# Later casts and subtractions for the second batch's turned queries and keys in a differential attention block

## The reference, cut to what matters

```
q = (query @ Wq).reshape(b, t, 32, 16);  k the same;  v = (query @ Wv).reshape(b, t, 16, 2, 16)
q = apply_rotary_interleaved(q, cos, sin);  k the same      # o1 = x1*c - x2*s, o2 = x1*s + x2*c
attn1 = softmax(causal(q1 k1^T * scale)) @ [v1, v2];  attn2 the same with q2, k2
attn  = irfft((rfft(attn1) - lambda * rfft(attn2)) * gaussian)   # along t
attn  = attn * rsqrt(mean(attn^2) + eps) * rms_weight * (1 - lambda_init)
x = x + attn.reshape(b, t, 512) @ Wout                      # then the other three blocks
```

## Time and profile before

| | us |
|---|---|
| median of 3 runs | 1260.25 (1258.77 to 1263.32) |
| profiled execution | 1260.45 |
| its span | 1258.7 |
| busy in the span: PE, DVE, ACT, POOL | 1127.6, 811.5, 618.0, 800.6 |
| busy from 180 to 900 us: PE, DVE, ACT, POOL | 629.26, 415.39, 440.50, 579.87 |

### The profile page before, as it was taken

How to read it: one execution, slowest core, us unless ns; L and a number is a source line. 1 busy time by engine, 2 the same in 40 slices (tenths; PEclk the granted TensorE clock), 3 DMA queues, 4 the chain that set the end, 5 groups by cost and what they waited for, 6 DMA issues and landing times. The chain is left out here.

```text
span 1258.7 us, 20791 instructions
## 1 busy us (share of the span) xinstructions
PE 1127.6 (90%) x7603; PEld 639.1 (51%) x7618; DVE 811.5 (64%) x1345; ACT 618.0 (49%) x1009; POOL 800.6 (64%) x584
## 2 busy tenths in 40 slices
PE   6999967989689889889898898897899999999996
PEld 5888722333234343343243243342367888887764
DVE  6887175565564665656557646643288788787786
ACT  4444215657557657656666564666642233332321
POOL 2012159569969879869879789668215677667321
PEclk9999959899889999999999998998999999999999
DMA  8333340120231220220221203103332322233651
GB/s 273 98 126 109 90 116 26 51 68 26 67 78 41 68 68 26 68 68 26 69 68 39 58 21 109 30 1 129 107 110 96 131 84 94 92 101 116 222 197 51
DMA packets 74836, 107.55 MB, mean 85 GB/s; under 512 B 12912, under 2 KB 36592, under 8 KB 74736
## 3 DMA queue, kind: packets, MB, share of 16 engines
q1 hardware_dynamic: 63616, 79.35, 21.4%
q0 software_dynamic: 4064, 14.16, 2.9%
q10 hardware_dynamic: 7056, 12.72, 2.7%
HBM read 68.44 MB, written 37.75 MB: 84 GB/s over the span
## 5 line engine op out<-in xcount | busy, mean ns | idle before, releaser
L1090 DVE TENSOR_REDUCE nm<-score 128x1 f32<-128x640 f32 (+6 forms) x352 | 349.4, 1025 | 272.6 <-PE score L981 220.8
L1257 POOL TENSOR_TENSOR base<-base,plain 128x2048 f32<-128x2048 f32 (+2 forms) x78 | 301.0, 3860 | 16.1 <-ACT plain L1206 6.2
L1206 ACT ACTIVATE plain<-score 128x1024 f32<-128x1024 f32 (+3 forms) x288 | 207.2, 734 | 108.4 <-PE score L997 60.4
L992 PE MATMUL score<-q,k 98*128 98x512 bf16 (+7 forms) x768 | 194.9, 340 | 51.7 <-ACT plain L1206 21.1
L992 PEld LDWEIGHTS score<-q,k 98*128 98x128 bf16 (+1 forms) x768 | 55.0, 99 | 155.1 <-DVE nm L1090 58.0
L1206 ACT ACTIVATE base<-score 128x1024 f32<-128x1024 f32 x96 | 97.5, 1023 | 72.9 <-PE score L997 51.6
L1010 PE MATMUL acc<-plain,vg 128*32 128x512 f32 (+3 forms) x1152 | 114.4, 470 | 0.0
L976 PE MATMUL score<-k,q 48*128 48x512 bf16 (+3 forms) x512 | 70.5, 355 | 17.7 <-DVE nm L1090 17.5
L1612 PE MATMUL m_b<-m_winh,m_hTh 128*128 128x512 f32 x192 | 83.6, 435 | 1.6 <-DVE m_k L1902 1.6
L1612 PE MATMUL m_b<-m_winh,m_hTl 128*128 128x512 f32 x192 | 75.8, 395 | 0.0
L1612 PE MATMUL m_b<-m_winl,m_hTh 128*128 128x512 f32 x192 | 75.7, 394 | 0.0
(11 more groups left out here) (312 smaller groups left out, 2514.3 us busy)
## 6 DMA issues: line engine op xcount, KB each, us to landing
q<-piece_scratch SPq DMA_DIRECT2D x192, 64.0 KB, 2.7
k<-piece_scratch SPq DMA_DIRECT2D x192, 64.0 KB, 2.3
piece_scratch<-n_pieces SPq DMA_DIRECT2D x16, 384.0 KB, 3.0
piece_scratch<-pieces POOLq DMA_DIRECT2D x8, 768.0 KB, 4.0
n_x1in<-in_query SPq DMA_DIRECT2D x16, 256.0 KB, 3.6
v_scratch<-n_v ACTq DMA_DIRECT2D x16, 256.0 KB, 2.2
vg<-v_scratch SPq DMA_DIRECT2D x8, 512.0 KB, 4.4
att_scratch<-m_qT SPq DMA_DIRECT2D x8, 512.0 KB, 3.0
```

The lines of the kernel that those rows point to most:

```text
L992: mm = nc.tensor.matmul(score[k % RING][:, x, t0:HALF], kst[n % SLOTS][c, first + x, j * P:(j + 1) * P], qst[n % SLOTS][c, first + x, h * ...
L1090: nc.vector.tensor_reduce(out, src, AX.X, ALU.max, negate=True).then_inc(s_max, 1)
L1206: nc.scalar.activation(tile_of(n, v)[:, first:first + 2, t0:HALF], score[k % RING][:, :, t0:HALF], ACT.Exp)\
L1257: nc.gpsimd.tensor_tensor(total, total, tile_of(n, v)[:, :, t0:HALF], ALU.add)\
```

## The change

Four of the five distances in `ROTATE` grow. Nothing else is altered, and every unit has the same operations as before.

```
-ROTATE = (('rotate', 0, 4), ('cast', 0, 12), ('rotate', 1, 15), ('cast', 1, 17), ('rotate', 2, 19))
+ROTATE = (('rotate', 0, 4), ('cast', 0, 14), ('rotate', 1, 17), ('cast', 1, 23), ('rotate', 2, 26))
```

## The result

Timed in turn with the kernel before, 20 executions each, the changed kernel takes 1266.1 us (1261.92 to 1267.7) and the kernel before 1258.93 us (1257.22 to 1263.86). The ratio is 1.0047, 95% interval 1.0036 to 1.0058: slower by 5.9 us, between 4.5 and 7.3 (the medians by themselves lie 7.2 us apart). That is resolved, and just within the 0.5%, 6.3 us, that the prediction called no change; the interval reaches past it. 1262.6 us was forecast, in a range from 1255 to 1268 us. The profiled execution took 1266.95 us, its span 1265.2 us, 6.5 us more than before.

A forecast was written before the change was run, and what follows sets the result against it. Bounds: POOL's unbroken row in even sets, waits for add 7 in sets 0 and 3, set 12's DMA. Terms -6.7 + 0.9 - 2.7 + 0 + 0.9 + 10.4 - 0.5 = +2.3 us give 1262.6 us, range 1255 to 1268 us.

The forecast's parts named there:

- Part 2 out of add 7's way, -6.7 us: Sets 0 and 3: POOL's last subtraction moves behind add 7, so v = 11 starts 3.43 and 3.26 us earlier.
- the clock in sets 0 and 3, -2.7 us: Behind v = 11, less idling ahead raises PE's granted clock: 2.1 us gained in set 0, 0.6 us in set 3.
- The collision with DVE's add, +0.9 us: Sets 0 and 3: the moved subtraction runs beside DVE's add and slows it by 0.43 us in each.
- The even sets, +0.9 us for POOL's idling: Behind add 5, POOL waits for rden before the output's product: 0 to 0.71 us a set, taken as 0.15, six times.
- The casts in the even sets, 0: Moving ACT's casts removes its stalls but gains nothing; at most 0.56 us a set, ending in a wait for add 1.
- The late DMA, +10.4 us: Set 12's DMA is issued 10.41 us later, so PE's wait for set 14's operands grows from 3.4 to 13.8 us.
- The clock behind that stall, -0.5 us: After PE's longer wait for set 14's operands, the lower clock changes by at most 2.7 us either way; -0.5 us taken.
- What the profile would show: Predicted signs: ACT's 28.4 us of waits gone, POOL's row unchanged, earlier outputs, PE's wait for set 14's operands 13 to 14 us.
- the third rival: Slower: set 12's late DMA counts fully, low clock stays in sets 0 and 3 and lasts longer behind the stall; 1268.5 us, chance 0.22.

The follow-up runs named there:

- kernels with spare matmuls: Unused matmuls added at PE's waits: set 12 old, other units new, 1253.66 us (only where PE idles, 1250.76 us); in the kernel before, 1258.9 us.
- the casts alone: Kernel before with only the casts moved later in sets 2, 4, 6, 8 and 10, POOL's order kept: 1259.34 us, ratio 0.9993.
- part 2 alone: Kernel before with only the last subtraction and its DMA moved later in sets 2, 4, 6, 8 and 10, casts as before: 1263.5 us, ratio 1.0029.
- sets 0 and 3 alone: Kernel before with only the units of sets 0 and 3 in the new order: 1253.69 us, ratio 0.9955.
- set 12 alone: Kernel before with only the unit of set 12 in the new order: 1267.88 us, ratio 1.0076.
- the first experiment: Changed kernel with set 12's unit back in its old order: 1252.78 us, ratio 0.9945; run a second time, 1256.84 us, ratio 0.9974.

## Why the prediction was right, and which of its terms were not

With the profiles of before, of after and of the experiments each stage can be compared over several executions with either order. Times are between POOL's output products; the stage of sets 0 and 1 begins at set 0's first one.

| stage | old order there | new order there | difference | forecast |
|---|---|---|---|---|
| sets 0 and 1 | 70.87, 68.12, 68.10, 68.09 | 64.88, 65.66, 64.86, 64.84 | -3.7 | -5.1 |
| sets 2 and 3 | 99.76, 99.74, 100.28 | 97.45, 97.32, 97.59, 97.41 | -2.5 | -3.3 |
| sets 4 to 11 | 355.07, 359.03, 357.78, 356.58 | 359.73, 355.81, 358.48 | +0.9 | +0.6 |
| set 12 | 53.84, 53.00, 55.06, 54.27, 53.56, 55.03 | 64.11, 64.07 | +10.0 | +10.05 |

The differences are of the means. The kernels with spare matmuls are left out; the kernel with the casts alone counts as old order, the one with part 2 alone stands only in the first and last row, and the one with sets 0 and 3 alone counts as new order in the second row, though its set 2 is old. The sum of the differences is +4.6 us (of the means before rounding); the timed ratio says +5.9 us, 4.5 to 7.3. Point by point:

- *Part 2 out of add 7's way, -6.7 us, and the clock in sets 0 and 3, -2.7 us:* both gains are there, but together they are some 6 us and not 9.4. In set 0, v = 11 starts 15.28 us behind the set's first output and no longer 18.50 us, as the first term says. The output behind it comes only 3.25 us earlier, though (26.2 us behind the first one instead of 29.4 us, three profiles of each order), and this holds the gain of the clock too. Three profiles show how it divides, from the first to the second output of set 0: the kernel before, set 12 alone (old order in set 0), and the changed one (first the length and PE's busy time, third from the end the granted clock).

```profile
202.35:233.21 30.86, 25.84 (x203) 9.42 (x202) 18.41 (x19) 15.72 (x21) 19.87 (x8) 0.89 0.18 54
```

```profile
199.87:229.27 29.40, 24.38 (x203) 9.14 (x202) 18.32 (x19) 15.68 (x21) 19.86 (x8) 0.94 0.15 48
```

```profile
202.28:228.47 26.19, 23.15 (x203) 8.63 (x202) 18.16 (x19) 15.72 (x21) 19.82 (x9) 1.00 0.16 51
```

PE has the same 203 matmuls. It idles 3.04 us instead of 5.02 us, 2.0 us less, and is busy 1.2 us less, at a granted clock of 1.00 instead of 0.94. The other profiles agree: with those with spare matmuls counted, the stretch was granted 0.94 in all four profiles that share the old order there with the kernel before, and 1.00 in five of six with the new one (0.94 in the first experiment). The clock that the kernel before had there in addition (0.89, 1.5 us more of busy time) was one execution's draw. In set 3, between its two outputs, the clock goes the same way, from 0.89 or 0.94 to 0.96 to 0.98. So the step that failed is this sum for set 0: a piece counted whole at 3.43 us, and on top of it a clock term of 2.1 us read from a single execution. They were worth 2.0 and 1.2 us. The changed kernel's profile gained 8.4 us up to set 3, as forecast, by that draw. The kernel with these two sets alone gained 5.7 us.
- *The collision with DVE's add, +0.9 us:* not paid. The subtraction ended at 219.53 us, and DVE's add began at 220.62 us with its undisturbed length:

```profile
220.62 1.75 DVE L1050 TENSOR_TENSOR base<-base,plain 128x1536 f32<-128x1536 f32 x1
```

I had priced the overlap without working out that there would be one. The Trainium skill's rule (SBUF — State Buffer, Who interferes with whom) had no case to act on between these two; set 3's add took 1.75 us as well.
- *The even sets, +0.9 us for POOL's idling:* the size was right, its cause was not. With the casts moved, POOL does not idle at all behind add 5; with them left it idles 0.8 us a set, a little over the upper bound of 0.71 us. What the new order costs is 0.15 us a set all the same (52.06 against 51.9 us for POOL's row), and it stands in the Newton step, which now starts earlier and lies otherwise against DVE's adds. Its first five operations take 8.60 to 8.63 us in sets 2 to 10 of the changed kernel and 8.45 to 8.48 us in the kernel before. Two of set 8's, beside the earlier trace rows:

```profile
584.12 2.58 POOL L1295 TENSOR_TENSOR m_sq<-m_sq,c 128x512 f32<-128x512 f32 x1
586.78 2.14 POOL L1296 TENSOR_TENSOR m_sq<-m_sq,m_k 128x512 f32<-128x512 f32 x1
```

- *The clock in sets 4 to 11, no term:* the profile's +4.7 us was nearly all this, and it is in part the order's doing. In sets 5, 7, 9 and 11 of the four profiles with the old order and no spare matmuls, PE waits 1.10 to 1.48 us for add 2, and the first denominator takes 1.06 or 1.07 us in all 16 cases. With part 2 late (the changed kernel, the first experiment twice, part 2 alone) PE waits 2.18 to 2.59 us there, and the denominator is slow, 1.32 to 1.94 us, in 10 of 16. Behind add 7 it is the other way round: POOL's wait for `rden` is above its undisturbed 5.64 us in 12 of 16 cases with the old order and in 1 of 16 with the new one. So with the new order the low clock is found at the one place in place of the other, and how often it falls there differs from one execution to the next. In the means the two nearly cancel, +0.9 us, from three and four profiles that differ by up to 4 us among themselves.
- *The casts in the even sets, 0:* right (0.9993), for the reason given: ACT's wait moved to PE's filter.
- *The late DMA, +10.4 us:* right, 10.3 us in the profile and 10.2 us by itself; PE's wait grew to 14.1 us, forecast as 13.8 us.
- *The clock behind that stall, -0.5 us:* nothing. The stretch behind the stall is at the lower clock for some 9 us in the changed kernel, and was for some 8.5 us before (0.50 from 770.6 us on, 0.61 from 776 to 780 us); here, the changed kernel's:

```profile
777.00:781.00 4.00, 3.94 (x26) 1.78 (x27) 2.06 (x3) 1.50 (x2) 0.00 (x0) 0.50 0.21 75
781.00:785.00 4.00, 4.00 (x24) 1.15 (x25) 1.94 (x2) 0.81 (x1) 0.00 (x0) 0.50 0.40 108
785.00:790.00 5.00, 4.73 (x56) 2.09 (x48) 1.65 (x2) 2.91 (x5) 1.55 (x2) 0.92 0.51 140
```

- *What the profile would show:* ACT's waits at v = 5 of the odd sets (1.46 instead of 0.32 us in set 9), the two outputs, POOL's row and PE's wait came as forecast, the last a hair above its 14 us. The output at 233.21 us is that of set 0's second half, not of set 1's first, as the prediction calls it; the reading of its time is not touched by this.

The forecast of a small loss was right in its mechanism, gains in sets 0 and 3 against one late DMA, and the DMA was its largest term. That the time came out as no change was close: +2.3 us was forecast and +5.9 us measured, and the third rival's +8.2 us is nearer to that. This rival named the right doubt, that the gains resting on the clock are too large, but not the right mechanism: sets 0 and 3 do not lie at the same low clock as before, and the clock behind the stall costs no 2.7 us. Without its two clock terms the forecast's sum would have been +5.5 us, and that it meets the +5.9 us so well is luck, for the clock's gain was real and the piece's was smaller.

What stays open: why the lower clock falls behind one such wait of 2.2 us and not behind another, with the same instructions in the same order around it. The runs show that it does and what it costs, not what decides it. As for how much of it there is, an estimate can be worked out from every execution's mean granted clock (twice the span times one minus the clock). The time at the lower level is 91.6 us in the mean of the changed kernel's 20 executions and 84 to 88 us in those of the kernel before. Some 10 us of that lie in the longer stall, where PE has nothing to do (the row below, of the changed kernel); the kernel with set 12 alone has 91.8 us against 85.1 us beside it. The kernel with sets 0 and 3 alone has 79.3 us against 87.7 us, which agrees with the clock's gain there.

```profile
767.00:777.00 10.00, 0.00 (x0) 0.00 (x0) 0.00 (x0) 0.00 (x0) 7.87 (x9) 0.50 0.54 160
```

The 1.3 us by which the table's sum falls short of the timed ratio are within its interval and within the scatter of the profiles; the runs do not say more.

## What to carry to other kernels

Before moving a step back in an engine's order, list everything that it issues and ask for each transfer who waits for it and whether that waiter has any reserve; here seven units had sets of time and the eighth none, so one table for all was the mistake, and that one unit cost 10 us. Do not size a gain from a clock state that was seen in a single execution: compare the stage over several before it enters a sum, and split what is gained into idle time and busy time of the limiting engine, or the same microsecond is counted twice. Where PE waits two or three microseconds in every pass, spare matmuls can hold the clock, but only there; at places where it does not wait they cost their full time.

## What the runs showed of the hardware

The order of instructions shows in where the lower clock falls, but does not decide whether it does: behind the same wait of PE in set 9 (2.2 us) the denominator's first eight matmuls took 1.06, 1.58 and 1.94 us in three profiles of the same order, and behind a wait of 1.1 to 1.5 us 1.06 or 1.07 us in all 16 cases. Over the executions of one kernel the total time moves with the time at the lower level (estimated as above), by 0.2 to 0.4 us for each us; the changed kernel took 1261.92 us at a mean clock of 0.967 and 1267.6 us at 0.961. Spare matmuls ahead of PE's waits go with less of it: 67.0 us against 79.7 us in the same kernel without them beside it, which had 73.8 us the first time. A DMA on the way from one engine to another, 768 KB out and 24 loads back, took 17.2 us from POOL's issue (753.40 us) to PE's going on (770.60 us) in the kernel before, and 11.0 us of this were the issue of the 24 loads one after the other.
